# Filter factor products on GpSimd, small VectorE operations in two-tensor forms, and ScalarE scalings in other places

## The reference, cut to what is computed

```python
x = u                                   # (8, 1024, 256) float32
xn = layernorm(x)                       # over the last axis, eps 1e-5
# filter: k[l, h] = Re sum_n W[h, n] exp(dt[h] (-exp(Lre[n]) + i Lim[n]) l), l < 128
s = causal_convolution(xn, k) + xn * D  # along the sequence, one filter per channel
gate = xq(xn) @ wq(w_gate).T            # xq, wq: FP4 quantised in blocks of 16
y = xq(xn) @ wq(w_up).T
g = silu(xq(silu(gate) * y) @ wq(w_down).T)   # hidden size 704
out = x + s * g
```

## Time and profile before

| | us |
|---|---|
| median of three runs (586.7 to 588.83) | 587.93 |
| the profiled execution | 586.48 |
| its span | 584.7 |
| VectorE (DVE) busy | 544.3, 93% of the span |
| PE busy | 473.7, 81% |
| ScalarE (ACT) busy | 407.2, 70% |
| GpSimd (POOL) busy | 198.4, 34% |

### The profile page before, as it was taken

One profiled execution on the slowest core, in us unless ns is written; L12 is line 12 of the kernel. 1 busy time (PEld: TensorE's weight loads), 2 busy tenths in 40 slices (PEclk: granted clock), 3 DMA queues, 4 the chain that ended last, 5 costly groups with the idle time before them and its releaser, 6 DMA issues.

```text
span 584.7 us, 13233 instructions
## 1 busy us (share of the span) xinstructions
PE 473.7 (81%) x4956; PEld 331.3 (57%) x4956; DVE 544.3 (93%) x689; ACT 407.2 (70%) x568; POOL 198.4 (34%) x302
## 2 busy tenths in 40 slices
PE   0000356668999999999999999999999999998965
PEld 0000234225555567777777777777777777765654
DVE  6999999989999999999999999999999999998884
ACT  6972866889988876767676767676767666664552
POOL 1094000474555551111111111333333333137870
PEclk9999957989999999999999999999999999999998
DMA  5990012225222335353534353535354535339978
GB/s 173 349 281 1 1 36 90 91 27 163 91 91 91 109 83 159 102 146 108 149 105 142 112 147 103 144 111 146 104 143 114 144 107 148 110 59 154 172 104 132
DMA packets 101186, 70.80 MB, mean 121 GB/s; under 512 B 8848, under 2 KB 100752, under 8 KB 101008
## 3 DMA queue, kind: packets, MB, share of 16 engines
q1 hardware_dynamic: 93072, 61.94, 35.8%
q0 software_dynamic: 8064, 8.13, 9.5%
HBM read 61.28 MB, written 16.91 MB: 134 GB/s over the span
## 4 chain that ended last, share of the span: by engine, by line
PE 57%; DVE 24%; issue 9%; POOL 6%; ACT 3%; DMA 0%; SPq 0%; DVEq 0%; POOLq 0%; ACTq 0%
PE ps L1224 27%; PE ps L1242 10%; PE ps L1244 5%; PE ps L1233 5%; PE ps L1257 4%; PE ps L1261 4%; DVE wgu L944 4%; DVE work L857 2%; DVE sm L799 2%; POOL gbuf L516 2%; DVE work L883 2%; PE ps L1212 2%; DVE work L852 2%; DVE xh L919 1%; DVE xh L912 1%
## 5 line engine op out<-in xcount | busy, mean ns | idle before, releaser
L1224 PE MATMUL ps<-wgu,work 128*128 128x512 f16 (+1 forms) x1152 | 242.7, 366 | 17.1 <-DVE work L883 15.9
L1224 PEld LDWEIGHTS ps<-wgu,work 128*128 128x128 f16 x1152 | 109.9, 99 | 128.0 <-issue 17.5
L615 ACT ACTIVATE work<-ps,con 128x704 f32<-128x704 f32 x64 | 54.2, 847 | 95.1 <-PE ps L1224 95.0
L1242 PE MATMUL ps<-wdh,work 128*128 128x256 f16 x704 | 87.9, 274 | 5.5 <-ACT gbuf L619 4.7
L610 ACT COPY work<-ps 128x1408 f16<-128x1408 f16 x64 | 84.7, 1325 | 2.1 <-PE ps L1233 1.9
L852 DVE SCALAR_TENSOR_TENSOR work<-work 128x960 f32<-128x960 bf16 (+2 forms) x67 | 71.8, 1110 | 1.6 <-ACT work L630 1.5
L1242 PEld LDWEIGHTS ps<-wdh,work 128*128 128x128 f16 x704 | 65.4, 98 | 13.4 <-issue 5.3
L516 POOL TENSOR_TENSOR gbuf<-gbuf,xh 128x256 f32<-128x256 f32 (+1 forms) x42 | 41.0, 1048 | 92.0 <-DVE work L865 77.8
L857 DVE SCALAR_TENSOR_TENSOR work<-work 128x1920 f16<-128x1920 bf16 (+3 forms) x36 | 69.7, 1936 | 1.2
L818 DVE TENSOR_TENSOR work<-work,ps 128x960 f32<-128x960 f32 (+2 forms) x63 | 68.4, 1126 | 1.1
L630 ACT ACTIVATE work<-work 128x960 bf16<-128x960 f32 (+2 forms) x67 | 61.8, 960 | 9.3 <-DVE work L818 8.7
(11 more groups left out here) (153 smaller groups left out, 675.1 us busy)
## 6 DMA issues: line engine op xcount, KB each, us to landing
work<-kpad SPq DMA_DIRECT2D x64, 512.0 KB, 3.8
work<-L_attn_u SPq DMA_DIRECT2D x33, 256.0 KB, 3.0
gbuf<-u_rev SPq DMA_DIRECT2D x4, 2048.0 KB, 18.6
out<-gbuf POOLq DMA_DIRECT2D x7, 1024.0 KB, 9.5
out<-L_attn_u SPq DMA_DIRECT2D x1, 768.0 KB, 5.5
out<-gbuf POOLq DMA_DIRECT2D x1, 768.0 KB, 8.1
work<-L_ffn_w_down SPq DMA_DIRECT2D x1, 704.0 KB, 6.6
work<-L_ffn_w_gate SPq DMA_DIRECT2D x1, 640.0 KB, 4.7
```

Source lines behind the costliest of these rows:

```text
L1224: last = T.matmul(p_gu[:, a:b], xT[par][:, t, c, :], wgu[:, part, c % 2, a:b], start=(n == 0), stop=(n == len(todo) - 1))
L1242: T.matmul(dst, hT[t][:, c, :], wdh[:, c, :], start=(c == 0), stop=False)
```

## The change

The two products go from VectorE to GpSimd, behind L534 and ahead of the memset of L537, and signal `k_af` there. On VectorE, tensor-scalar operations of the norm and the constants become operations with a second tensor: a constant column in SBUF (`k_cs` and five more, filled by memsets near L903), spread over the width where needed; one halving of `mean` is folded into a factor of a later operation (-1.0 becomes -0.5). `mxo` and `mrow` move from SBUF to PSUM. On ScalarE the odd scalings 7 to 13 move behind high(0), `weights_out` and the copies, only 15 stays in step 1, and the count that `a_high` waits for in steps 0 and 1 grows by one. ScalarE waits for `k_af` ahead of `high(0)`, which writes over what the second product reads.

```diff
--- before.py
+++ after.py
@@ -278,7 +278,9 @@
         rn_r = lasting(2 * NT)
         lim, lre = lasting(1), lasting(1)
         phi = lasting(4)
-        mxi, mxo, mp2, minv, mrow = (lasting(4) for _ in range(5))
+        mxi, mp2, minv = (lasting(4) for _ in range(3))
+        k_cs, k_xs, k_half, k_eps, k_gate, k_floor = (lasting(1) for _ in range(6))
+        mxo, mrow = (ps[:, 3824 + 4 * i:3828 + 4 * i] for i in range(2))
         mean, va, sq0, rq = (early[:, 1792 + NT * (6 + i):1792 + NT * (7 + i)] for i in range(4))
         xflat = xh[:, :, :, :, :].rearrange("p q a t c -> p (q a t c)").bitcast(F32)
         uu = xflat[:, 0:8192].rearrange("p (r h) -> p r h", r=32)
@@ -533,7 +535,16 @@
             own.settle()
             nc.gpsimd.tensor_tensor(uu[:, 16:24, :], uu[:, 16:24, :], uu[:, 24:32, :], ALU.add).then_inc(k_aw, 1)
 
-            pool.wait_ge(k_af, 1)
+            pool.wait_ge(k_aw, 1)
+            pool.wait_ge(k_sin, 28)
+            a1 = uu[:, 16:24, :]
+            own.mark(nc.gpsimd.tensor_tensor(amat.rearrange("p (g h r) -> p r h g", g=16, r=FA),
+                                             a1.rearrange("p r (h g) -> p r h g", g=16),
+                                             kk[:, 16:24, :].rearrange("p r (h g) -> p r h g", g=16), ALU.mult))
+            own.settle()
+            nc.gpsimd.tensor_tensor(fmat, uu[:, 0:16, :].rearrange("p r (h g) -> p (r h) g", g=16),
+                                    kk[:, 0:16, :].rearrange("p r (h g) -> p (r h) g", g=16), ALU.mult
+                                    ).then_inc(k_af, 1)
             nc.gpsimd.memset(sd_lo[:, :, I:RT * P], 0.0).then_inc(w_pad, 1)
 
             todo = [(n, part) for n in range(FIRST) for part in range(len(PARTS))]
@@ -670,7 +681,7 @@
                 if a2:
                     if not first:
                         a_scale(it * 2)
-                    scaled = it + 7 if isinstance(it, int) and it < 2 else it + (NT // 8 + 1)
+                    scaled = it + 8 if isinstance(it, int) and it < 2 else it + (NT // 8 + 1)
                     a_high(it * 2, scaled)
                     a_high(it * 2 + 1, scaled)
                 if td:
@@ -714,8 +725,8 @@
             a_scale(1)
             act.wait_ge(ln_ok, 1)
             x_norm(0, 0)
-            for n in range(1, 6):
-                a_scale(2 * n + 1)
+            a_scale(3)
+            a_scale(5)
 
             def weights_out(ns):
 
@@ -729,17 +740,22 @@
                 act.wait_ge(w_g, m + 1)
                 nc.scalar.copy(gu_hi[m], wraw[:, W_COLS[m]]).then_inc(w_h, 1)
 
+            act.wait_ge(k_af, 1)
             high(0)
             act.wait_ge(k_pad, 32)
             x_norm(1, 1)
+            a_scale(7)
             high(1)
             weights_out(range(0, 6))
             square(-2, 1, True, False, 0)
             weights_out(range(6, 8))
+            a_scale(9)
             x_copy(0, 0)
+            a_scale(11)
             act.wait_ge(w_g, 3)
             for k in range(2):
                 nc.scalar.copy(dn_hi[k], dn_src).then_inc(w_h, 1)
+            a_scale(13)
             square(-1, 0, True, False, 0)
             weights_out(range(8, 11))
             x_norm(2, 0)
@@ -750,8 +766,7 @@
             for it in range(PEEL):
                 step(it, it % 2, True, it >= 1, True, True, it >= 1, it >= 2, a2=True, td1=it >= 3, first=it >= 1)
                 if it == 1:
-                    for n in range(6, 8):
-                        a_scale(2 * n + 1)
+                    a_scale(15)
             with act.Fori(0, (S_CONV - PEEL) // 2) as q:
                 for par in range(2):
                     step(q * 2 + (PEEL + par), par, True, True, True, True, True, True, a2=True)
@@ -901,6 +916,9 @@
                 own.mark(V.memset(phi[0:64, r:r + 1], a))
                 own.mark(V.memset(phi[64:128, r:r + 1], b))
             own.mark(V.memset(phi[:, 3:4], MAGIC))
+            for column, value in ((k_cs, CS), (k_xs, XS), (k_half, 0.5), (k_eps, EPS), (k_gate, XS ** -2 / SHRINK),
+                                  (k_floor, TINY * XS ** 2 * SHRINK)):
+                own.mark(V.memset(column, value))
             own.mark(V.memset(con[:, C_ROUND:C_ROUND + 1], C0))
             own.settle()
             dve.wait_ge(k_exp, 2)
@@ -960,9 +978,8 @@
             own.mark(V.tensor_tensor(rq, half[:, :, 1], half[:, :, 4], ALU.subtract))
             own.mark(V.tensor_tensor(va, half[:, :, 2], half[:, :, 5], ALU.add))
             own.settle()
-            own.mark(V.tensor_scalar(mean, mean, 0.5, None, ALU.mult))
             own.mark(V.scalar_tensor_tensor(rq, rq, 0.25, rq, ALU.mult, ALU.mult))
-            own.mark(V.tensor_scalar(va, va, 1.0 / H, EPS, ALU.mult, ALU.add))
+            own.mark(V.scalar_tensor_tensor(va, va, 1.0 / H, k_eps.to_broadcast([P, NT]), ALU.mult, ALU.add))
             own.settle()
             V.tensor_tensor(va, va, rq, ALU.add).then_inc(v_ok, 1)
 
@@ -976,14 +993,15 @@
 
             dve.wait_ge(w_all, 1)
             powers(slice(0, 3))
-            own.mark(V.tensor_scalar(con[:, C_GATE:C_GATE + 1], mp2[:, 0:1], XS ** -2 / SHRINK, None, ALU.mult))
-            own.settle()
-            own.mark(V.tensor_scalar(con[:, C_FLOOR:C_FLOOR + 1], minv[:, 1:2], TINY * XS ** 2 * SHRINK, None, ALU.mult))
-            own.mark(V.tensor_scalar(con[:, C_DOWN:C_DOWN + 1], mp2[:, 1:2], mp2[:, 2:3], (XS * XS * SHRINK) ** -2, ALU.mult, ALU.mult))
+            own.mark(V.tensor_tensor(con[:, C_GATE:C_GATE + 1], mp2[:, 0:1], k_gate, ALU.mult))
+            own.settle()
+            own.mark(V.tensor_tensor(con[:, C_FLOOR:C_FLOOR + 1], minv[:, 1:2], k_floor, ALU.mult))
+            own.mark(V.scalar_tensor_tensor(con[:, C_DOWN:C_DOWN + 1], mp2[:, 1:2], (XS * XS * SHRINK) ** -2, mp2[:, 2:3],
+                                            ALU.mult, ALU.mult))
             dve.wait_ge(w_v, 2)
             for m, (a, b) in enumerate(W_MATS):
-                ins = V.tensor_scalar(wrs[:, a:b], wbm[:, a:b], minv[:, m:m + 1], XS, ALU.mult, ALU.mult)
-                own.mark(ins)
+                own.mark(V.scalar_tensor_tensor(wrs[:, a:b], wbm[:, a:b], minv[:, m:m + 1], k_xs.to_broadcast([P, b - a]),
+                                                ALU.mult, ALU.mult))
 
             dve.wait_ge(q_ok, 1)
             own.mark(V.reciprocal(rq, sq0))
@@ -992,30 +1010,19 @@
             own.settle()
             own.mark(V.tensor_tensor(rq, rq, sq0, ALU.add))
             own.settle()
-            own.mark(V.tensor_scalar(rq, rq, 0.5, None, ALU.mult))
+            own.mark(V.tensor_tensor(rq, rq, k_half.to_broadcast([P, NT]), ALU.mult))
             own.settle()
             own.mark(V.reciprocal(rn_r[:, 0:NT], rq))
             own.settle()
-            own.mark(V.tensor_scalar(rs_c, rn_r[:, 0:NT], CS, None, ALU.mult))
-            V.scalar_tensor_tensor(rn_r[:, NT:2 * NT], mean, -1.0, rn_r[:, 0:NT], ALU.mult, ALU.mult
+            own.mark(V.tensor_tensor(rs_c, rn_r[:, 0:NT], k_cs.to_broadcast([P, NT]), ALU.mult))
+            V.scalar_tensor_tensor(rn_r[:, NT:2 * NT], mean, -0.5, rn_r[:, 0:NT], ALU.mult, ALU.mult
                                    ).then_inc(rn_ok, 1)
             dve.wait_ge(rn_ok, 1)
-            V.tensor_scalar(nm_c, rn_r[:, NT:2 * NT], CS, None, ALU.mult).then_inc(nm_ok, 1)
+            V.tensor_tensor(nm_c, rn_r[:, NT:2 * NT], k_cs.to_broadcast([P, NT]), ALU.mult).then_inc(nm_ok, 1)
 
             dve.wait_ge(fl_ok, 1)
             own.mark(V.tensor_copy(rstd[:], ps[:, 0:NT]))
             V.tensor_copy(nmr[:], ps[:, NT:2 * NT]).then_inc(ln_ok, 1)
-
-            dve.wait_ge(k_aw, 1)
-            a1 = uu[:, 16:24, :]
-            dve.wait_ge(k_sin, 28)
-            own.mark(V.tensor_tensor(amat.rearrange("p (g h r) -> p r h g", g=16, r=FA),
-                                     a1.rearrange("p r (h g) -> p r h g", g=16),
-                                     kk[:, 16:24, :].rearrange("p r (h g) -> p r h g", g=16), ALU.mult))
-            own.settle()
-            V.tensor_tensor(fmat, uu[:, 0:16, :].rearrange("p r (h g) -> p (r h) g", g=16),
-                            kk[:, 0:16, :].rearrange("p r (h g) -> p (r h) g", g=16), ALU.mult
-                            ).then_inc(k_af, 1)
 
             def round_matrix(m):
```

## The result

The changed kernel takes 591.64 us (median of 4 runs, 591.12 to 592.35) against 587.32 us for the kernel before (median of 4 runs, 586.40 to 588.83): a ratio of 1.0077, with a 95% interval from 1.0057 to 1.0096. So it is 0.8% slower. Its profiled execution took 591.12 us with a span of 589.3 us, 4.6 us above the 584.7 of before. Executions of one kernel scatter with the mean clock that TensorE was granted (of 29 of the kernel before, the 12 at 0.970 or more took 586.12 to 587.05 us, the 12 at 0.966 or less 587.36 to 588.84); the two profiled ones compared here both had 0.971.

What follows compares the result with a forecast made beforehand. VectorE, busy 96% of the loop, was taken as the bound. Holds of 4.0 + 9.2 us, 8.2 saved and 0.2 for what passes between gave +4.8: 586.48 + 4.8 = 591.3, against the median 592.7 us, range 588.8 to 596.8.

Steps and rivals of the forecast that it cites:

- The products' lengths: On GpSimd in the set-up, the first product would take 4.5 us from 51.1 and the second 9.0 us.
- rival of the slow first product: GpSimd's strided writes stretch the first product to 7.4 us, everything slides by 2.9, 595.6 us; chance 12%.
- The wait in their place: VectorE's small operations wait for GpSimd's whole products: L959 about 4.1 us, one of L960, L961 or L964 about 9.
- port shared at half speed: Rival: the port is shared, not held, so rounding beside the second product loses some 3.5 us; 584.4 us, chance 3%.
- Working it out: VectorE's set-up chain: second product ends 64.8, L961 to chain end takes 5.65 us, first rounding at 70.5 against 65.74.
- 4.0 + 9.2 us held: Check of VectorE's delay: these holds, 8.2 us saved and 0.2 for what passes between, against 4.8 us late.
- What bounds the loop: VectorE is busy 96% of the loop, so a delay in the set-up is paid in full at the end.
- ScalarE's part: Moved scalings fit ScalarE's gaps and cost nothing; first scaling at 69.5, x block at 84.4, 0.2 us of cover thin.
- The forms: In VectorE's chain, the dropped halving gains 0.1 us; two-tensor forms give about that back or 0.2 us more.
- The sum: Whole kernel: 586.48 + 4.8 = 591.3 us, or 592.7 us against the median of the runs shown.
- about the same sum: If more small operations passed before the second product, it would end later by as much and hold the rounding instead.

Runs made afterwards that it cites:

- run 1: Changed kernel with two-tensor forms put back to tensor-scalar, mxo and mrow back in SBUF, products still on GpSimd: 592.25 us, ratio 1.0073 to the kernel before.
- run 4: Changed kernel with small VectorE operations beside the products taking at most one input from SBUF, using PSUM and three more small instructions: 586.01 us, ratio 0.9975.
- run 6: Changed kernel with only the first product on GpSimd, the second back on VectorE behind the copies of rstd and nmr: 586.66 us, ratio 0.9990.
- run 10: Kernel before with the new two-tensor forms, products on VectorE, plus eight 960-column GpSimd memsets beside the small operations: 588.03 us, ratio 1.0014.
- run 2: Kernel before with only the constants, two-tensor forms, folded halving and mxo and mrow in PSUM, products on VectorE: 587.82 us, ratio 1.0006.
- run 3: Kernel before with only ScalarE's part of the change, its scalings spread and its wait on k_af: 587.29 us, ratio 0.9996.
- run 5: Changed kernel with GpSimd's second product cut into eight instructions of 512 columns: 591.3 us, ratio 1.0062 to the kernel before.
- run 8: Changed kernel with only the first product and 1024 columns of the second on GpSimd, small operations' operands in PSUM as in run 4: 583.11 us, ratio 0.9921.
- run 9: Kernel before with its tensor-scalar forms, products on VectorE, plus eight 960-column GpSimd memsets beside the small operations: 589.17 us, ratio 1.0032.

## Why the prediction was right

The forecast was 592.7 us (588.8 to 596.8), slower with 77%; the median is 591.64. By its steps:

- **The products' lengths.** Forecast 4.5 and 9.0 us, measured 4.52 and 8.90. The stride of the writes cost GpSimd nothing that shows (4.52 against 4.51 for the dense sum before it), though it cost VectorE 1.46 us (3.75 against 2.29). The rival of the slow first product falls.
- **The wait in their place.** Forecast: L959 about 4.1 us, one of its neighbours about 9 us. Measured 4.04 and 8.88. Runs 1, 4 and 6 confirm the holding from three sides: with the old forms other operations bear it (4.20 and 8.69 us), with one input in PSUM none does until the rounding (8.07), and with the first product alone only its part is left (4.04). Beside GpSimd's memsets, which read nothing, two-tensor operations with both inputs in SBUF are not held (run 10: 0.22 to 0.25 us on 64 columns). The variant of a port shared at half speed falls too: it would make 3.5 us of the 1.76 of run 4's rounding, not 8.07. By what the two engines hold each other, no run shows.
- **Working it out.** Forecast for the rounding 70.5, measured 70.31: 0.1 us is the second product's length, the rest the chain, 5.57 us from the end of L979 to the rounding instead of 5.65. Here two small errors met, and that they cancel is luck. The forecast took the 5.65 us from the start of L961, though a held sum is done when its record ends; from its end (51.96 + 0.25) it is 5.40. And it reckoned with nothing net for the forms and the dropped halving (or 0.2 us more), where they cost 0.17 us in this stretch. In the same way its 4.0 + 9.2 us held contain the sums' own time: beyond their 0.25 us each, L977 and L979 stood for 3.79 + 8.63 = 12.42 us. Less the 8.13 saved, and with the 0.22 of run 2, that is 4.51 of the 4.57 us.
- **What bounds the loop.** The forecast paid the delay in full because VectorE is busy for 96% of the loop. The same row has PE busy for 364.20 of its 369.00 us, 99%, and the chain that ended last in the kernel before runs mostly through PE:

```profile
PE 57%; DVE 24%; issue 9%; POOL 6%; ACT 3%; DMA 0%; SPq 0%; DVEq 0%; POOLq 0%; ACTq 0%
```

  That the delay arrives in full held (4.57 us at the first x block, 4.6 in the span); the reason given for it is not the one that the profile shows, and no run tells which of the two engines bounds the loop.
- **ScalarE's part.** Forecast nothing, and a first scaling at 69.5, low(1) unhindered, x block at 84.4. Measured 69.38 and 84.16; run 3 alone shows no difference. The cover of 0.2 us before x_copy held.
- **The forms.** Forecast a gain of 0.1 and a loss of as much or 0.2 more; run 2 shows a loss of 0.2 us net. Reading PSUM for mxo and mrow, put at nothing beyond 0.1 us, starts the first sum 0.12 us late; beside GpSimd's product, which holds that sum anyhow, this is hidden.
- **The sum.** +4.8 us forecast, +4.6 in the span and 4.3 between the medians. The forecast stands 1.1 us above the median: 0.2 us is in the step for the rounding, 0.6 in the median of before (587.93 of three runs as shown, 587.32 with a fourth), the rest is scatter.

What I had not right: that more of the small operations passing before the second product would leave "about the same sum" holds for operations that take turns with GpSimd, as in run 1. In run 4, where none does, the second product ends as early (64.54) and VectorE's second rounding instruction starts at 66.19 instead of 72.10. And what I expected of run 5, one to three operations at each boundary, came of reading more into the earlier trace rows than they show.

## What to carry to other kernels

Before moving work from VectorE to GpSimd, list what VectorE does meanwhile, and count each operation that takes both inputs from SBUF, and each tensor-scalar operation or copy from SBUF to SBUF. In these runs the first of them beside a GpSimd instruction that reads SBUF stood until that one ended, even on 64 columns (4.04 us instead of 0.25) or on three rows (4.20 instead of 0.21), and the profile shows it as a long small instruction and not as a wait. The move paid where those operations took one input from PSUM, and GpSimd's share was cut to end when VectorE next needed two inputs from SBUF (run 8: 583.11 us against 587.95, with the first product and a quarter of the second moved). Changing tensor-scalar into two-tensor forms helped only beside GpSimd's memsets, which read nothing (589.17 us in run 9, 588.03 in run 10).

## What the runs showed that I had not expected

- With GpSimd's instructions back to back, one held VectorE operation passed per GpSimd instruction, even an operation on one column (1.18 us for L1000; run 5: eight parts of about 1.25 us, eight held operations; one more, on one column, passed behind a held one).
- A GpSimd memset held VectorE's tensor-scalar operations from SBUF to SBUF on 64 columns (0.20 us become up to 0.90 in run 9) and left two-tensor operations alone (0.22 to 0.25 us in run 10). So in these runs writing alone held the one kind of VectorE instruction, and the other was held only beside instructions that read as well (4.04 and 8.88 us in the changed kernel).
- Writes with a step of 128 words cost VectorE 1.46 us on 2048 columns (3.75 against 2.29) and GpSimd nothing that shows (4.52 against 4.51).
- The holding goes the other way too, and the kernel before shows it outside the tail: in step 1, GpSimd's L491 on 88 columns takes 2.25 us (from 117.93) beside VectorE's rounding L857 (117.83 to 119.99), which has both inputs in SBUF; in the loop, beside L818, which reads PSUM, it takes 0.33 us (at 404.56).
